# Half of a small per-sample mixing matmul on 32-row tiles, and the last output piece stored in two halves

## The reference

```python
w = weights[conditions]                       # [32, 32, 32]
y = einsum('bct,bcd->bdt', x, w)              # x is [32, 32, 256]
h = silu(y @ w_gate) * (y @ w_up)             # [.., 1024]
h_sparse = of each 4 neighbours of h, keep the 2 largest in magnitude
out = x + h_sparse @ w_down                   # [32, 32, 256], f32
```

## Time and profile before

| | before |
|---|---|
| median of 3 runs | 81.5 us (81.41 to 81.61) |
| the profiled execution | 81.4 us, its span 79.6 us, granted clock 1.00 |
| TensorE matmuls | 74.6 us (94% of the span), 333 |
| TensorE weight loads | 59.3 us (74%), beside the matmuls |
| VectorE | 61.3 us (77%), 89 |
| ScalarE | 41.6 us (52%), 61 |
| GpSimd | 8.6 us (11%), 18 |
| HBM read, written | 5.38 MB, 1.05 MB |

### The profile page before, as it was taken

One profiled execution on the slowest core, in us unless ns is written; L12 is line 12 of the kernel. 1 busy time (PEld: TensorE's weight loads), 2 busy tenths in 40 slices (PEclk: granted clock), 3 DMA queues, 4 the chain that ended last, 5 costly groups with the idle time before them and its releaser, 6 DMA issues.

```text
span 79.6 us, 960 instructions
## 1 busy us (share of the span) xinstructions
PE 74.6 (94%) x333; PEld 59.3 (74%) x333; DVE 61.3 (77%) x89; ACT 41.6 (52%) x61; POOL 8.6 (11%) x18
## 2 busy tenths in 40 slices
PE   3998999999999999999999999999999999999920
PEld 1336888879888888888888888888888888888800
DVE  0017691699879999599999979999999999992330
ACT  6130853769353375599897679697370504700000
POOL 5550000000000013000804000006000000000000
PEclk9999999999999999999999999999999999999999
DMA  0848559983910004900199990004992000006303
GB/s 1 268 161 212 216 156 374 419 356 78 403 66 0 0 0 80 183 0 0 35 196 200 191 175 6 4 0 91 177 206 54 0 0 0 0 0 241 125 30 132
DMA packets 3076, 9.62 MB, mean 121 GB/s; under 512 B 480, under 2 KB 480, under 8 KB 2816
## 3 DMA queue, kind: packets, MB, share of 16 engines
q1 hardware_dynamic: 2144, 6.29, 21.9%
q0 software_dynamic: 928, 3.28, 21.6%
HBM read 5.38 MB, written 1.05 MB: 81 GB/s over the span
## 4 chain that ended last, share of the span: by engine, by line
PE 87%; DMA 5%; DVE 2%; issue 1%; DVEq 0%
PE bank L527 51%; PE bank L564 14%; PE y_banks L564 14%; PE y_banks L512 5%; PE bank L538 4%; DMA h<-in_table,rows_sb 3%; DMA cond_sb<-in_cond 2%; DVE gate_raw L417 1%; DVE h L342 1%; DVE h L333 1%; DVE rows_sb L421 0%; DVEq L416 0%; DVEq L340 0%
## 5 line engine op out<-in xcount | busy, mean ns | idle before, releaser
L527 PE MATMUL bank<-y_hl,up_hl 128*128 128x512 f32 x96 | 24.2, 389 | 0.0
L527 PE MATMUL bank<-y_hl,gate_hl 128*128 128x512 f32 x84 | 21.4, 390 | 0.0
L527 PEld LDWEIGHTS bank<-y_hl,up_hl 128*128 128x128 f32 x96 | 18.0, 188 | 3.8
L527 PEld LDWEIGHTS bank<-y_hl,gate_hl 128*128 128x128 f32 x84 | 15.7, 188 | 3.2
L229 ACT ACTIVATE silu<-bank 128x512 f32<-128x512 f32 x16 | 9.6, 597 | 12.5 <-PE bank L527 12.3
L367 DVE TENSOR_TENSOR h<-bank,silu 128x512 f32<-128x512 f32 x12 | 8.3, 688 | 4.6 <-ACT silu L229 4.5
L564 PE MATMUL y_banks<-h_hl,down_hl 128*128 128x512 f32 x48 | 11.0, 389 | 0.0
L564 PE MATMUL bank<-h_hl,down_hl 128*128 128x512 f32 x48 | 11.0, 389 | 0.0
L564 PEld LDWEIGHTS y_banks<-h_hl,down_hl 128*128 128x128 f32 x48 | 9.0, 188 | 1.9
L564 PEld LDWEIGHTS bank<-h_hl,down_hl 128*128 128x128 f32 x48 | 9.0, 188 | 1.9
L250 ACT ACTIVATE h_hl<-h 128x1024 fp32r<-128x1024 f32 (+1 forms) x8 | 6.7, 842 | 3.9 <-DVE h L403 3.9
(11 more groups left out here) (40 smaller groups left out, 67.8 us busy)
## 6 DMA issues: line engine op xcount, KB each, us to landing
h_hl<-h POOLq DMA_DIRECT2D x4, 512.0 KB, 6.1
x_sb<-in_x SPq DMA_DIRECT2D x2, 512.0 KB, 3.3
up_raw<-in_w_up SPq DMA_DIRECT2D x2, 512.0 KB, 5.0
down_raw<-in_w_down SPq DMA_DIRECT2D x1, 1024.0 KB, 8.1
gate_raw<-in_x_t SPq DMA_DIRECT2D x1, 1024.0 KB, 5.1
down_hl<-down_raw POOLq DMA_DIRECT2D x2, 512.0 KB, 4.8
out<-gate_raw SPq DMA_DIRECT2D x4, 256.0 KB, 2.3
gate_raw<-in_w_gate SPq DMA_DIRECT2D x2, 256.0 KB, 3.2
```

Source lines behind the costliest of these rows:

```text
L527: last = nc.tensor.matmul(dst, w_hl[w][:, s, q, k, j], y_hl[:, m, half, k], start=i == 0, stop=i == len(terms) - 1)
```

## The change

1. **Mixing of the first 128 columns of T (half 0, k = 0)** is no longer made with the block diagonal but batch by batch: 16 matmuls with 32 rows each (`mixing_by_batch`), stationary `x_sb[rows, g, 0:128]`, moving the 32 columns of `mix_w`. Batch b uses the rows 32b to 32b + 31 and writes bank b, so that each row tile has a bank of its own. The other three quarters of the mixing stay on the block diagonal.
2. **Banks:** all eight are one tensor. The ring's pairs are (4, 0), (5, 1), (2, 3), the `y_banks` 6 and 7; k = 0 of the first half is mixed in banks 0 to 3. `high_y` and `low_y` read it from there with the batches interleaved.
3. **Warm-up:** 12 matmuls instead of 13.
4. **Output:** the last piece (half 1, k = 1) is added in two halves of 256 columns. The first is stored by SyncE, the second by ScalarE.
5. **Waits:** on TensorE the wait for the first high gate weights stands in front of the mixing instead of the first gates; on VectorE the wait for the marks of the diagonal stands in front of the first transpose, and that for x_t in front of all outputs instead of in each.

```diff
-    WARM_START = 13
+    WARM_START = 12
...
+        banks = ctx.enter_context(nc.psum_tensor("banks", [P, 8, TH], f32))
+
+        GATE_BANKS, UP_BANKS = [4, 5, 2], [0, 1, 3]
+        y_banks = banks[:, 6:6 + KT]
...
+        def mixed_y(half, k, end):
+            if (half, k) == (0, 0):
+                return banks[:, 0:NB, 0:GH * D].rearrange("p b (i d) -> p i b d", i=GH)
+            return y_banks[:, k:end].rearrange("p k (i b d) -> p (k i) b d", b=NB, d=D)
...
-        OUTPUTS = [(half, k) for half in range(NH) for k in range(KT)]
+
+        OUTPUTS = [(0, 0, 0, TH), (0, 1, 0, TH), (1, 0, 0, TH), (1, 1, 0, TH // 2), (1, 1, TH // 2, TH)]
...
-            for i, (half, k) in enumerate(OUTPUTS):
-                cols = slice(half * TH, (half + 1) * TH)
+            for i, (half, k, begin, end) in enumerate(OUTPUTS[:-1]):
+                cols = slice(half * TH + begin, half * TH + end)
                 sp.wait_ge(out_done, i + 1)
                 sp.dma_start(out[:, k, cols], xt_sb[:, k, cols]).then_inc(stored, 16)
...
-                nc.scalar.activation(y_hl[:, HI, half, k:end], y_banks[:, k:end], ACT.Copy).then_inc(y_hi, 1)
+                nc.scalar.activation(split_y(HI, half, k, end), mixed_y(half, k, end), ACT.Copy).then_inc(y_hi, 1)
...
             high_h(3, 3, 4)
+            half, k, begin, end = OUTPUTS[-1]
+            cols = slice(half * TH + begin, half * TH + end)
+            act.wait_ge(out_done, len(OUTPUTS))
+            act.dma_start(out[:, k, cols], xt_sb[:, k, cols]).then_inc(stored, 16)
...
-                dve.wait_ge(blocks_marked, 1 + NB)
                 dve.wait_ge(transposed, half + 1)
...
-                dve.wait_ge(xt_in, 16)
-                dve.wait_ge(down_done, i + 1)
-                nc.vector.tensor_tensor(xt_sb[:, k, cols], down_bank(half, k), xt_sb[:, k, cols],
+                dve.wait_ge(down_done, KT * half + k + 1)
+                nc.vector.tensor_tensor(xt_sb[:, k, cols], down_bank(half, k)[:, begin:end], xt_sb[:, k, cols],
...
+            dve.wait_ge(blocks_marked, 1 + NB)
             transpose_rows(0)
...
+            dve.wait_ge(xt_in, 16)
             for i in range(len(OUTPUTS)):
                 output(i)
...
+            def mixing_by_batch():
+
+                pe.wait_ge(x_in[0], 16)
+                pe.wait_ge(transposed, 1)
+                for g in range(GH):
+                    for b in range(NB):
+                        rows = slice(b * C, (b + 1) * C)
+                        last = nc.tensor.matmul(banks[:, b, g * D:(g + 1) * D], x_sb[rows, g, 0:P],
+                                                mix_w[rows, g, 0], start=True, stop=True)
+                last.then_inc(mixed, 1)
...
-                    pe.wait_ge(w_hi if s == HI else w_lo, pieces_until(0, 0, k))
+                    if i > 0:
+                        pe.wait_ge(w_hi if s == HI else w_lo, pieces_until(0, 0, k))
...
             warm_up(WARM_START)
-            mixing(0)
+            pe.wait_ge(w_hi, pieces_until(0, 0, 0))
+            mixing_by_batch()
+            mixing(0, 1)
             first_gates()
```

More of the change, by code:

```diff
@@ L83, in adaln_ffn @@
         count = sb("count", [P, M, TH], bf16)
-        ring = [ctx.enter_context(nc.psum_tensor(f"bank{i}", [P, TH], f32)) for i in range(2 * RING)]
-        y_banks = ctx.enter_context(nc.psum_tensor("y_banks", [P, KT, TH], f32))
+        banks = ctx.enter_context(nc.psum_tensor("banks", [P, 8, TH], f32))
+        GATE_BANKS, UP_BANKS = [4, 5, 2], [0, 1, 3]
+        y_banks = banks[:, 6:6 + KT]
         cond_in = sem("cond_in")
@@ L126, in gate_bank, with split_y @@
         def gate_bank(n):
-            return ring[2 * (n % RING)]
+            return banks[:, GATE_BANKS[n % RING]]
         def up_bank(n):
-            return ring[2 * (n % RING) + 1]
+            return banks[:, UP_BANKS[n % RING]]
+        def mixed_y(half, k, end):
+            if (half, k) == (0, 0):
+                return banks[:, 0:NB, 0:GH * D].rearrange("p b (i d) -> p i b d", i=GH)
+            return y_banks[:, k:end].rearrange("p k (i b d) -> p (k i) b d", b=NB, d=D)
+        def split_y(part, half, k, end):
+            return y_hl[:, part, half, k:end].rearrange("p k (i b d) -> p (k i) b d", b=NB, d=D)
         def down_bank(half, k):
-            return y_banks[:, k] if half == 0 else (gate_bank(ACC_PAIR), up_bank(ACC_PAIR))[k][:]
+            return y_banks[:, k] if half == 0 else (gate_bank(ACC_PAIR), up_bank(ACC_PAIR))[k]
         Y_PIECES = [(0, k, k + 1) for k in range(KT)] + [(1, 0, KT)]
@@ L228, in gate_silu @@
                     act.wait_ge(h_done, n - 2)
-                nc.scalar.activation(silu[:, n % 3], gate_bank(n)[:], ACT.Silu).then_inc(silu_done, 1)
+                nc.scalar.activation(silu[:, n % 3], gate_bank(n), ACT.Silu).then_inc(silu_done, 1)
             def absolute(n):
@@ L355, in low_y @@
                 dve.wait_ge(y_hi, i + 1)
-                nc.vector.tensor_tensor(y_hl[:, LO, half, k:end], y_banks[:, k:end],
-                                        y_hl[:, HI, half, k:end].bitcast(f32), ALU.subtract).then_inc(y_lo, 1)
+                nc.vector.tensor_tensor(split_y(LO, half, k, end), mixed_y(half, k, end),
+                                        split_y(HI, half, k, end).bitcast(f32), ALU.subtract).then_inc(y_lo, 1)
             def product(n):
@@ L366, in product @@
                     dve.wait_ge(h_lo_sent[0][j // 2], 16)
-                nc.vector.tensor_tensor(hs[u][:, j], up_bank(n)[:], silu[:, n % 3],
+                nc.vector.tensor_tensor(hs[u][:, j], up_bank(n), silu[:, n % 3],
                                         ALU.mult).then_inc(h_done, 1)
@@ L412, in output @@
             def output(i):
-                half, k = OUTPUTS[i]
-                cols = slice(half * TH, (half + 1) * TH)
-                dve.wait_ge(xt_in, 16)
-                dve.wait_ge(down_done, i + 1)
-                nc.vector.tensor_tensor(xt_sb[:, k, cols], down_bank(half, k), xt_sb[:, k, cols],
+                half, k, begin, end = OUTPUTS[i]
+                cols = slice(half * TH + begin, half * TH + end)
+                dve.wait_ge(down_done, KT * half + k + 1)
+                nc.vector.tensor_tensor(xt_sb[:, k, cols], down_bank(half, k)[:, begin:end], xt_sb[:, k, cols],
                                         ALU.add).then_inc(out_done, 1)
@@ L499, in warm_up, with mixing @@
                 for _ in range(times):
-                    nc.tensor.matmul(ring[0][:], warm[:, 0:P], warm[:], start=True, stop=True)
-            def mixing(half):
+                    nc.tensor.matmul(gate_bank(0), warm[:, 0:P], warm[:], start=True, stop=True)
+            def mixing_by_batch():
[7 more added lines that the diff above has]
+                last.then_inc(mixed, 1)
+            def mixing(half, first=0):
                 pe.wait_ge(x_in[half], 16)
@@ L505, in mixing @@
                     pe.wait_ge(y_lo, KT * half)
-                for k in range(KT):
+                for k in range(first, KT):
                     for i in range(GH):
@@ L509, in mixing @@
                         span = [groups.start <= g < groups.stop for groups in SPANS].index(True)
-                        if k == 0 and g == SPANS[span].start:
+                        if k == first and g == SPANS[span].start:
                             pe.wait_ge(diag_done, span + 1)
@@ L534, in first_gates @@
                 for i, (s, m, k) in enumerate(terms):
-                    pe.wait_ge(w_hi if s == HI else w_lo, pieces_until(0, 0, k))
+                    if i > 0:
+                        pe.wait_ge(w_hi if s == HI else w_lo, pieces_until(0, 0, k))
                     pe.wait_ge(y_hi if m == HI else y_lo, k + 1)
                     for n in (0, 1):
-                        nc.tensor.matmul(gate_bank(n)[:], w_hl[0][:, s, 0, k, n], y_hl[:, m, 0, k],
+                        nc.tensor.matmul(gate_bank(n), w_hl[0][:, s, 0, k, n], y_hl[:, m, 0, k],
                                          start=i == 0, stop=i == len(terms) - 1)
@@ L548, in gate_up @@
                         continue
-                    last = split_product(dst[:], w, q, half, j)
+                    last = split_product(dst, w, q, half, j)
                 last.then_inc(pair_done, 1)
```

## The result

| | before | changed |
|---|---|---|
| median of 12 runs | 81.56 us (81.39 to 81.81) | 80.99 us (80.87 to 81.40) |
| ratio | | 0.994 (95% interval 0.9928 to 0.9953) |
| the profiled execution's span | 79.6 us | 79.2 us |

The change is 0.57 us faster by the medians, and 0.49 us by the ratio (0.006 of 81.56; the interval is 0.38 to 0.59). The forecast was 80.9 us, 0.6 faster. Medians in this text take in every execution, the ratios leave out those over 1.5% above the fastest of their kernel (here there was none).

The account below looks back on a forecast made before the run. TensorE was taken as the bound, with 87% of the chain that ended last. From the profiled 81.4 us, 0.33 (front) and 0.24 (end) off gave 80.8, and 0.1 for the runs' median made 80.9 us, range 80.6 to 81.9.

Parts of the forecast that it names:

- The start of the strips: Front: batchwise mixing needs the transpose alone and starts 0.15 us behind it, at 6.18, 0.53 earlier than before.
- The price of a strip record: Mixing of the first 128 columns: all four row strips load side by side, 0.028 us a record, 0.89 for 32.
- Rival 1: Mixing: strips pair up only, 0.056 us a record; front 0.37 to 0.66 lost, 81.6 to 81.9 us; chance 0.20.
- no row here bears on either: Mixing: no profile row was said to bear on the skill's load overlap by row group or strip matmuls 4 ns apart.
- The pause at the change of tiles: Before and behind the strips: TensorE may drain at each change, 0.2 to 0.3 us ahead of the second half.
- The front: Start of kernel up to the first gate matmul: 0.33 us won, taken between 0.21 with drains and 0.43 without.
- The upper bound: First gates: the second gate weights, landed at 8.3, allow no useful start before 8.19 instead of 8.62, 0.43 us won.
- The three waits: Moved waits on TensorE and VectorE: nothing waits for them; the x_t one takes some 0.02 us out of the end.
- The end: Behind the last matmul: last piece added and stored in halves, packets end at 78.40 instead of 78.65, 0.24 us won.
- The packets: Last store: packets shrink from 2048 to 1024 B, drawn on to 0.05 us each instead of 0.087.
- The sum: Whole kernel: 81.4 less 0.33 and 0.24 is 80.8; with the runs' median 0.1 above, 80.9 us.
- rival 3: Behind the last matmul: the end gives nothing or takes 0.4 us, the front holds; 81.1 to 81.6 us; chance 0.11.

Follow-up runs that it names:

- experiment 3: Changed kernel with the batch loop outside and the group loop inside, so eight records in a row use the same 32 rows: 84.01 us, ratio 1.0289 to before.

## Why the prediction was right

**The start of the strips.** Foreseen 0.15 behind the transpose, found 6.39 to 6.53, 0.14. The 0.53 of lead over the diagonal is real, where the warm-up is out of the way. One reading beside it was wrong and did no harm: the weight load at 5.86 in the earlier trace rows is the thirteenth's; the twelfth matmul starts at the same 5.86.

**The price of a strip record.** Taken at 0.028, measured 0.027; this choice of one in three decided the sign. Its reason (different rows, a bank for each) was not enough: experiment 3 has both and runs at 0.071. Rival 1 had named the right danger, the order in which loads are taken, but not what decides: two records in a row on a strip cost nothing (0.027), eight do (0.071); no number between was tried. The Trainium skill (TensorE: Matmul & The Clock Gate, Part 3) pairs a load's overlap with running matmuls with differing row groups. For loads beside loads this case shows the same: 0.027 apart where neighbours differ. The prediction's "no row here bears on either" was wrong for the page's "only": in the earlier trace rows loads of 128 rows start 0.11 apart from 6.68 on beside matmuls on the same 128 rows from 6.71 on.

**The pause at the change of tiles.** The last strip load starts at about 7.33; a full load would come 0.11 behind it, at 7.44, and the first one starts at 7.55: 0.11 of pause. From the mixing to the gates, full array both, there is none (8.33 to 8.44). In front of the strips it is 0.13 (6.43, the end of the last warm-up's columns, to 6.56, in the profile with the marks back). I had 0.2 a change as one bound and none as the other. The Trainium skill (TensorEngine Tiling (Array Packing), Tiling Modes) says that a change of mode drains TensorE. The pause agrees in kind, but the full load of 7.55 starts before the last strip matmul's record ends at 6.53 + 1.09 = 7.62; since such ends are modelled, the trace can't tell whether the array was empty.

**The front** was put at 0.33, between 0.21 and 0.43, and is 0.45 from the gather on; with the marks' wait left behind the transpose it is 0.51 (3.01 to 2.50). So the value was too low, and the 0.08 of the moved wait hid a part of that. The upper bound, set by the second gate weights' landing, was right as a mechanism: in the profiles with 2.50 and 2.49 the first gate starts before it, but the twelve gates then lose 0.07 and 0.16 to it, which leaves 0.44 and 0.36. In the changed kernel's two profiles it rules in one (0.22) and not in the other.

**The three waits** is the step that failed. "Nothing waits for either" is true of the semaphores, which had long been given. But a second wait costs a step of its own, and ahead of the transpose that step stood on the gather's path: 0.08 us, in every one of the nine profiles with the moved wait, and 0.01 in the five without. The same step left the second mixing, where it was worth about 0.05 (5.50 or 5.51 with it, 5.44 to 5.46 without, one profile with late up weights apart), and the last addition, where it was worth 0.07 and not the 0.02 that I took from one sequencer row. Three moves of one step: 0.08 lost, 0.05 and 0.07 won.

**The end** was put at 0.24 and is 0.19, of which the halves bring 0.12, half of what was forecast for them: two additions take 0.07 more than one, as counted, but ScalarE's store lands 2.05 behind its issue, not 1.93. The packets: 1024 B were drawn at 0.05 and the stretch of both stores shows 277 GB/s at a share of 0.83, 20.9 GB/s an engine, 0.049:

```profile
77.20:77.70 0.50, 0.00 (x0) 0.00 (x0) 0.00 (x0) 0.00 (x0) 0.00 (x0) 1.00 0.83 277
```

ScalarE's issue takes 0.37, near SyncE's 0.33, and could have been left to SyncE.

**The sum** of 0.57 against 0.49 to 0.57 is right partly by chance: the parts seen in the trace add up to 0.69, and losses go off it in some executions: a late landing of the second gate weights (0.07 to 0.22 in four of ten profiles) or of the first up weights (0.22 in one), and a warm-up that still runs at the lower level (0.42 and 0.48 in two). The first was in the prediction. The last was not: I had read the warm-up from one execution, in which the level rose at the eleventh matmul, and took twelve to be out of the way always. How often each occurs, one or two profiles of each kernel can't tell, and a gather that lands later in the changed kernels, which the parts leave out by their starting point, is not ruled out either. What makes up the difference of 0.12 to 0.20 stays open.

Two chances were added wrongly: the rest of rival 3 and half of rival 1 are 0.155, not 0.18, which leaves 0.245 for slower, not 0.22. Nothing hung on it.

## What to carry to other kernels

Small matmuls on different row strips run fully side by side only if they are neighbours in the program; let the strips take turns, and look at the spacing of the weight loads, not at the number of matmuls. A wait that has long been fulfilled still costs a sequencer step if the instruction has another wait, so it belongs in front of an instruction that is not on the path. And before a stage is pulled forward against a warm-up, read the warm-up's end in the execution where the clock rises last.

## What the runs showed of the hardware

- Thirty-two weight loads of 32 rows and 128 f32 columns start 0.027 us apart when four strips take turns, 0.071 when eight in a row are on one strip, against 0.111 for 128 rows.
- Going over from strips to the full array leaves a pause of 0.11 us on top of the usual 0.11 between loads; from the last warm-up's columns to the strips it is 0.13 us.
- The granted clock stood at 0.50 from 9.5 to 12.9 us, with matmuls back to back, behind 2.4 us of strips in poor order.
- Matmuls of 256 float32r columns are 0.120 apart, those of 512 0.227: half of it and 0.0065.
- A second semaphore, long given, on VectorE's transpose delays it by 0.08 us behind the landing that it waits for.
- The mean granted clock of an execution does not read the warm-up: it reads 1.00 over warm-ups 0.43 us apart, and what lowers it to 0.994 lies behind the last matmul.
- Store packets of 1024 B take 0.049 us an engine, of 2048 B 0.087.
